# First feed forward: the rows of batches 2 and 3 come back beside the second attention's first groups, in a ring of four buffers

## The chip, the cores and the metric

One core of a Trainium2 chip runs the whole program. The metric is the device time of one execution in microseconds (us), here the median of the runs. Engines: TensorE (PE, matrix products), VectorE (DVE), ScalarE (ACT), GpSimd (POOL) and SyncE (SP, which issues DMAs). Each works through its own queue in order, and semaphores tie the queues together. SBUF is the memory that the engines work in, PSUM (eight banks) receives what TensorE makes.

## What is computed

Four layers on x of shape (4 batches, 1024 rows, 128), each with a layer norm ahead and a residual:

```
x = x + attention_a(layernorm(x))      # 8 heads of 128, relative positions
x = x + feed_forward(layernorm(x))     # 8 experts, top 2
x = x + attention_b(layernorm(x))      # 16 query heads of 8, one key/value head, causal
x = x + feed_forward(layernorm(x))     # the same weights

def feed_forward(x):                   # per row
    scores = softmax(x @ Wg.T);  top 2 of 8, shares renormalised to p1, p2
    for the two experts e:
        a, b = split(x @ W1[e].T + b1[e]);  g = a * sigmoid(b)       # 256 wide
        out += p_e * (g @ Wo.T + bo)
```

## The kernel before

The 4096 rows are 32 tiles of 128 rows (n = 0 to 31), eight to a batch. Three plans, lists of units, give the order: `plan_a` (first attention, with the routing of the first feed forward), `plan_f(0, opening)` followed by the order of the second attention from `plan_b`, and `plan_f(1, [])`. Every engine walks the same list and does its own part of each unit, so the order of the list is the order of each engine's queue.

**The feed forward** sorts rows by expert. `m_disp` scatters normalised rows to DRAM (`xsd`) by an indirect DMA of POOL. `m_load` and `m_turn` bring sorted tiles back and turn them, `m_mm` multiplies a pair of tiles with the expert's weights (TensorE), takes the gate (tanh on ScalarE, m_sig; VectorE, m_gg), and `m_store` writes the pair to DRAM (`gsd`, SP's queue). There are three parts: batches 0 and 1 (20 pairs), batch 2 (12) and batch 3 (12), 44 pairs in all. Then the rows come back, for each tile n:
- `m_gath`: POOL issues two indirect DMAs (one for each of the two experts) into a buffer of a ring. The first gather of a part waits until the part's last four pairs are stored. The ring has `NP` = 7 buffers, and it is the memory of `P`, the attention's probabilities (line 570 on: `self.gb = self.P...`).
- `m_sum`: ScalarE scales the first half (m_acc, line 1215), VectorE adds the second (line 1593). It waits for the gather.
- `m_fin`: TensorE turns m_acc (2 transposes, line 914), ScalarE copies (m_th, 1223), VectorE takes the rest (m_tl, 1598).
- `m_proj`: TensorE multiplies with Wo (6 matmuls, lines 927 to 929), VectorE adds to x (line 1604).

In `plan_f` a set `back(n)` = m_sum n, m_fin n-1, m_proj n-2 follows a pair from pair 24 on, one set for 1.1 pairs. That is sets 0 to 17 by the last pair; the rest stands in a list that `spread` mixes with the opening of the second attention, and the last unit of it is `("b_zero", 1)`, POOL's memset of the key buffer K1. K1 and Q1 lie on the memory of the first feed forward's own buffers (gg, sig, acc, th, tl, xn), so they can be written only when it is through.

**The second attention** has 16 groups (4 batches x 4 groups of 4 heads). The opening makes inputs and keys of batch 0 (`b_in`, `b_keys`), values (`b_vals`), the row maxima of group 0 (`b_max`, 48 of them: TensorE line 1088, VectorE lines 1800 and 1804), and the shift of the queries by them (`b_shift`, `b_shift2`). Group n then has scores (`b_s`, TensorE line 1109), exponentials (ScalarE, 1354), masks (POOL, 760), products with the values (`b_pv`, 1127), and `b_norm`; beside it run the maxima of group n+1 and the inputs of group n+2. `in_order` makes the order: each line of units has due times in groups; of the units that are next in their lines it takes the one with the least idle time by its model of engines, latencies and banks, plus `SLACK` (4000 ns) for each group that it is due later than the earliest. Maxima use banks 0 to 2, scores 3 to 5, products 6, and everything else bank 7.

The second attention's first exponential waits for the last m_sum, since the ring of gathers lies in P:

```
elif nst == 1:
    e.wait_ge(S["b_wlo"], 1)
    e.wait_ge(S["m_sum"], NT)
e.activation(self.P[:, pt, off:512], ps[:, bank, off:512], ACT.Exp).then_inc(S["b_exp"], 1)
```

Of the kernel before, what the change touches and what calls it, by code (L numbers as in the profile page):

```python
# [26 lines left out]
NP = 7  # L27
LATENCY = {"PE": 200, "ACT": 120, "DVE": 150, "POOL": 120, "DMA": 0}
SLACK = 4000.0
NEG = -1e30  # L30
# [146 lines left out]
def plan_f(f, more):  # L177
# [56 lines left out]
def plan_b():  # L234
# [55 lines left out]
    line("scores", tail, 16, 16)  # L290
    rows = disp(1, 0) + disp(1, 1)
# [8 lines left out]
def in_order(lines, due):  # L300
# [5 lines left out]
    def steps(u):  # L306
# [67 lines left out]
        if kind == "m_bias":  # L374
            return [("DVE", 2300, [], [])]
        return [("DVE", 1200, [], [])]
# [14 lines left out]
    def allowed(u):  # L391
# [8 lines left out]
        if kind == "b_in" and u[2] == 4:  # L400
            return ("xb_bias", u[1]) in done
        if kind == "ln_stats":
            return ("b_out2", u[2], 1) in done if u[1] == 3 else True
# [38 lines left out]
class Program:  # L442
# [27 lines left out]
    def memory(self):  # L470
# [93 lines left out]
        self.gb = self.P[:, :, :].rearrange("p s (k n) -> p s k n", k=2)  # L564
        for f in range(2):
            with ExitStack() as c:
# [6 lines left out]
                self.xn8.append(buf("xn", [128, 8, 128]))  # L573
            self.K.append(sb(f"K{1 - f}", [128, 4, L], F32R))
# [208 lines left out]
    def gpsimd_routed(self, e, u):  # L783
# [19 lines left out]
        elif u[0] == "m_gath":  # L803
# [6 lines left out]
            if i == 0:  # L810
                e.wait_ge(S["b_wlo"], 1)
            if i >= NP:
                e.wait_ge(S["m_sum"], i - NP + 1)
            for k in range(2):
                e.indirect_dma_start(self.gb[:, i % NP, k, :], None, self.gsd[part],
                                     bass.IndirectOffsetOnAxis(self.slot[:, k, n:n + 1], 0)).then_inc(self.d_gath[i % NP], 16)
# [351 lines left out]
    def scalar_side(self, e, u):  # L1168
# [40 lines left out]
        elif u[0] == "m_sum":  # L1209
            _, f, n = u  # L1210
            i = NT * f + n
            e.wait_ge(self.d_gath[i % NP], 32 * (i // NP + 1))
# [726 lines left out]
```

## Time and profile before

| what | us |
|---|---|
| median of 3 runs | 2677.29 (2676.71 to 2681.56) |
| profiled execution | 2673.23 |
| its span in the trace | 2671.5 |
| PE busy | 2431.9 (91%) |
| DVE busy | 1891.9 (71%) |
| ACT busy | 1547.2 (58%) |
| POOL busy | 438.9 (16%) |

Stages on the trace's clock: first attention to 1571, first feed forward to 1722, opening of the second attention to 1788, its groups to about 2490, second feed forward to the end.

How to read the rows: "1750.38 0.48 DVE L1593" is a start, a duration, an engine and a line of the kernel. A bracket at the end gives the idle time before it and what ended it. PE is TensorE's matmuls, PEld its weight loads. Matmul records overlap (each is longer than the distance to the next), so a busy PE is not a full one, and the cost of an instruction in a full queue is the distance to the next start. A releaser "remote" is one that the profile can't name. PEclk is the granted clock of TensorE as a share of full speed.

### The profile page before, as it was taken

The numbers are of one execution on the slowest core, as the hardware profiler recorded it, in microseconds if no ns is written. First come the engines' busy times: TensorE is split into PE (matmuls) and PEld (weight loads), VectorE is DVE, ScalarE is ACT, GpSimd is POOL, SyncE is SP. The second block draws the span as 40 slices with busy tenths as digits, with TensorE's granted clock in tenths as the row PEclk, the third lists the DMA queues.
The fourth block names the chain that finished last, engine by engine and source line by source line (L and its number), as shares of the span: only waits on it lengthen the run. The fifth ranks groups of instructions, "written<-read, shape, count | busy, mean of one in ns | idle before, by whom it ended". The sixth has DMA issues, their size and how long they took to land.

```text
span 2671.5 us, 40400 instructions
## 1 busy us (share of the span) xinstructions
PE 2431.9 (91%) x13240; PEld 1878.4 (70%) x13240; DVE 1891.9 (71%) x4726; ACT 1547.2 (58%) x3107; POOL 438.9 (16%) x825
## 2 busy tenths in 40 slices
PE   4999898999999999999999977789999989988776
PEld 3788787788888888888888855665555545544655
DVE  4677776777877778777777754588887877873544
ACT  3566565666766656666566633537766656555333
POOL 0000011000000012000020005422222223423154
PEclk9999999999999999999999987879999989999786
DMA  4666578666666667666577625400000000000363
GB/s 139 238 227 226 185 252 289 212 205 224 230 223 231 206 216 242 213 230 220 200 240 244 225 84 176 147 20 1 1 1 1 1 9 10 24 5 13 110 191 117
DMA packets 171554, 402.51 MB, mean 151 GB/s; under 512 B 28226, under 2 KB 85186, under 8 KB 171010
## 3 DMA queue, kind: packets, MB, share of 16 engines
q1 hardware_dynamic: 154578, 360.38, 40.1%
q0 software_dynamic: 12208, 35.62, 4.3%
q10 hardware_dynamic: 4560, 3.93, 0.5%
q8 instruction: 108, 1.77, 0.3%
q14 instruction: 100, 0.82, 0.1%
HBM read 208.88 MB, written 193.66 MB: 151 GB/s over the span
## 4 chain that ended last, share of the span: by engine, by line
PE 74%; DVE 11%; ACT 5%; issue 4%; another core or an unknown queue 2%; DMA 2%; POOL 1%; SPq 0%; DVEq 0%; ACTq 0%; POOLq 0%
PE ps L1015 7%; PE ps L432 7%; PE ps L434 7%; PE ps L433 7%; PE ps L1088 5%; PE ps L1127 5%; PE ps L990 5%; PE ps L989 5%; PE ps L1109 4%; PE ps L1028 4%; PE ps L1030 4%; PE ps L1029 4%; DVE ps L1800 2%; DVE r_mx L1804 1%
## 5 line engine op out<-in xcount | busy, mean ns | idle before, releaser
L1305 ACT ACTIVATE a_Ph<-ps 128x512 fp32r<-128x512 f32 x512 | 304.9, 596 | 443.0 <-PE ps L1015 440.4
L1354 ACT ACTIVATE r_P<-ps 128x512 f32<-128x512 f32 (+3 forms) x768 | 329.5, 492 | 194.2 <-PE ps L1109 183.0
L1702 DVE CUSTOM_DVE_ANT_0 a_sp<-ps,a_sp 128x1024 f32<-128x1024 f32 x256 | 313.0, 1223 | 144.6 <-PE ps L434 123.6
L1708 DVE TENSOR_TENSOR a_Pl<-ps,a_Ph 128x512 fp32r<-128x512 f32 x512 | 348.8, 682 | 9.8 <-ACT a_Ph L1305 9.8
L989 PE MATMUL ps<-a_fa,a_ua 128*128 128x384 f32 (+2 forms) x960 | 328.0, 354 | 20.5 <-ACT a_rt L1290 18.4
L1298 ACT ACTIVATE a_sp<-a_sp,a_nm 128x1024 f32<-128x1024 f32 x256 | 295.0, 1152 | 50.2 <-DVE a_nm L1702 49.4
L1015 PE MATMUL ps<-ident,a_sp 128*128 128x128 f32 x2048 | 308.9, 274 | 0.0
L1015 PEld LDWEIGHTS ps<-ident,a_sp 128*128 128x128 f32 x2048 | 257.6, 141 | 71.2 <-issue 1.4
L1088 PE MATMUL ps<-r_K,r_Q 128*128 128x512 f32 (+3 forms) x768 | 280.0, 406 | 28.3 <-DVE r_mx L1800 14.3
L990 PE MATMUL ps<-a_fb,a_ub 86*128 86x384 f32 (+2 forms) x960 | 290.7, 318 | 0.0
L1800 DVE CUSTOM_DVE_ANT_0 ps<-ps,r_maskq 128x256 f32<-128x256 f32 (+3 forms) x512 | 244.3, 504 | 38.8 <-PE ps L1088 36.5
L1290 ACT ACTIVATE a_rt<-ps 128x384 f32<-128x384 f32 x512 | 251.1, 490 | 23.3 <-DMA scr<-a_rt 12.7
L1109 PE MATMUL ps<-r_Q,r_K 128*128 128x512 f32 (+3 forms) x768 | 251.5, 383 | 8.7 <-ACT r_P L1354 6.5
L1088 PEld LDWEIGHTS ps<-r_K,r_Q 128*128 128x128 f32 x768 | 145.3, 198 | 145.0 <-DVE r_mx L1800 73.8
L801 POOL DMA_INDIRECT xsd<-m_xd,m_slot x96 | 93.7, 976 | 900.8 <-issue 507.1
L1028 PE MATMUL ps<-a_Ph,a_nath 128*128 128x512 f32 x512 | 215.7, 421 | 27.1 <-DVE a_Pl L1708 26.9
L760 POOL TENSOR_SCALAR_AFFINE_SELECT r_P<-r_P 128x128 f32<-128x128 f32 x512 | 152.5, 309 | 420.4 <-ACT r_P L1354 412.4
L432 PE MATMUL ps<-p_xh,a_gah 128*128 128x512 f32 x512 | 208.3, 407 | 2.5 <-DVE a_ub L1676 1.6
L434 PE MATMUL ps<-p_xh,a_gal 128*128 128x512 f32 x512 | 206.2, 403 | 0.0
L433 PE MATMUL ps<-p_xl,a_gah 128*128 128x512 f32 x512 | 205.5, 401 | 0.0
L989 PEld LDWEIGHTS ps<-a_fa,a_ua 128*128 128x128 f32 x960 | 184.8, 193 | 29.1 <-ACT a_rt L1290 22.4
L1030 PE MATMUL ps<-a_Ph,a_natl 128*128 128x512 f32 x512 | 203.6, 398 | 0.0
(248 smaller groups left out, 4872.9 us busy)
## 6 DMA issues: line engine op xcount, KB each, us to landing
scr<-a_rt SPq DMA_DIRECT2D x256, 576.0 KB
a_sp<-scr SPq DMA_DIRECT2D x256, 512.0 KB, 4.6
gsd<-m_gg SPq DMA_DIRECT2D x82, 256.0 KB
a_share<-rdr SPq DMA_DIRECT2D x64, 256.0 KB, 4.7
a_wc<-wsp SPq DMA_DIRECT2D x24, 512.0 KB, 5.5
m_sx<-xsd SPq DMA_DIRECT2D x38, 256.0 KB
wsp<-a_wc SPq DMA_DIRECT2D x8, 512.0 KB, 5.6
xsd<-in_q POOLq DMA_DIRECT2D x2, 1472.0 KB, 18.5
```

What stands on the lines that cost most here:

```text
L432: e.matmul(out, lh, rh, start=True, stop=False)
L433: e.matmul(out, lh, rl, start=False, stop=False)
L434: return e.matmul(out, ll, rh, start=False, stop=True)
L989: e.matmul(out, self.ua[:, s, side, qs], self.fa[:, base + a:base + z], start=True, stop=False)
L990: i = e.matmul(out, self.ub[:, s, side, qs], self.fb[:, base + a:base + z], start=False, stop=True)
L1015: i = e.transpose(ps[:, 4 + j % 2, 128 * k:128 * k + 128], self.sp[:, (4 * qd + k) % NSP, 128 * j:128 * j + 128], ident[:, :])
L1028: e.matmul(OB, self.nath[:, s, j, :], self.Ph[:, slot, :], start=j == 0, stop=False)
L1088: e.matmul(ps[:, bank, 0:w], self.Q[b % 2][:, g, 128 * I:128 * I + 128], self.K[b % 2][:, q, 512 * part:512 * part + w], start=True, stop= ...
L1109: e.matmul(ps[:, bank, off:512], self.K[b % 2][:, q, 128 * J:128 * J + 128], self.Q[b % 2][:, g, 512 * ch + off:512 * ch + 512], start=Tru ...
L1354: e.activation(self.P[:, pt, off:512], ps[:, bank, off:512], ACT.Exp).then_inc(S["b_exp"], 1)
L1702: e.tensor_tensor_reduce(out=w, in0=ps[:, 2:4, :].rearrange("p a n -> p (a n)"), in1=w, scale=-1.0, scalar=3e38, op0=ALU.add, op1=ALU.min, ...
L1708: e.tensor_tensor(self.Pl[:, n % 2, :], ps[:, 4 + n % 2, :], self.Ph[:, n % 2, :].bitcast(F32), ALU.subtract).then_inc(S["p_lo"], 1)
```

## The change

The gathers of the first feed forward get four buffers of their own (`gb0`, in the memory that K1 and Q1 use later); the second feed forward keeps seven in P. `plan_f(0)` stops at tile 16 (batches 0 and 1). Tiles 16 to 31 come back in a new line "back" of the second attention, due over groups 0 to 2.2, with gathers three tiles ahead and m_fin and m_proj in bank 7; the memset of K1 is its last unit. `in_order` learns costs for these units, and that inputs of batch 1's keys come after the memset. The first exponential no longer waits for m_sum.

```
+NG = (4, 7)
+SPILL = 16
@@ plan_f
+    end = NT if f else SPILL
     for part in range(2):
-        side.setdefault(last[part], []).extend(("m_gath", f, n) for b in PARTS[part] for n in range(8 * b, 8 * b + 8))
+        side.setdefault(last[part], []).extend(("m_gath", f, n) for b in PARTS[part] for n in range(8 * b, 8 * b + 8) if n < end)
     def back(n, fin, proj):
-        return [u for u in (("m_sum", f, n), ("m_fin", f, n - 1, fin), ("m_proj", f, n - 2, proj)) if 0 <= u[2] < NT]
+        return [u for u in (("m_sum", f, n), ("m_fin", f, n - 1, fin), ("m_proj", f, n - 2, proj)) if 0 <= u[2] < end]
-    p += [("m_gath", f, n) for n in range(8 * B - 8, 8 * B)]
-    rest = [u for n in range(nb, NT + 2) for u in back(n, 3 + n % 2, 5)]
+    p += [("m_gath", f, n) for n in range(8 * B - 8, end)]
+    rest = [u for n in range(nb, end + 2) for u in back(n, 3 + n % 2, 5)]
     rest.insert(len(rest) // 2, ("m_bias", f, B - 1))
-    if f == 0:
-        rest.append(("b_zero", 1))
+
+def rows_back(f, lo, ahead):
+    r = [("m_gath", f, n) for n in range(lo, min(lo + ahead, NT))]
+    for n in range(lo, NT + 2):
+        r += [u for u in (("m_sum", f, n), ("m_fin", f, n - 1, 7), ("m_proj", f, n - 2, 7)) if lo <= u[2] < NT]
+        r += [("m_gath", f, n + ahead)] * (n + ahead < NT)
+    return r + [("b_zero", 1)]
@@ plan_b
     line("scores", tail, 16, 16)
+    line("back", rows_back(0, SPILL, 3), 0, 2.2)
@@ in_order: steps
+        if kind == "m_gath":
+            return [("POOL", 2540, [("gb", u[2] % 4)], []), ("DMA", 2600, [], [("got", u[2])])]
+        if kind == "m_sum":
+            return [("ACT", 350, [("got", u[2]), ("acc", u[2] % 2)], [("half", u[2])]),
+                    ("DVE", 400, [("half", u[2])], [("gb", u[2] % 4), ("sum", u[2])])]
+        if kind == "m_fin":
+            return [("PE", 260, [("bank", 7), ("sum", u[2])], [("pe", 0), ("acc", u[2] % 2)]), ("ACT", 320, [("pe", 0)], [("hi", 0)]),
+                    ("DVE", 340, [("hi", 0)], [("bank", 7), ("tl", u[2])])]
+        if kind == "m_proj":
+            return [("PE", 650, [("bank", 7), ("tl", u[2])], [("pe", 0)]), ("DVE", 200, [("pe", 0)], [("bank", 7), ("x", u[2] // 8)])]
+        if kind == "b_zero":
+            return [("POOL", 4000, [], [])]
@@ in_order: allowed
         if kind == "b_in" and u[2] == 4:
-            return ("xb_bias", u[1]) in done
+            return ("xb_bias", u[1]) in done and ("b_zero", 1) in done
@@ gpsimd_routed
-            if i == 0:
-                e.wait_ge(S["b_wlo"], 1)
-            if i >= NP:
-                e.wait_ge(S["m_sum"], i - NP + 1)
+            if n >= NG[f]:
+                e.wait_ge(S["m_sum"], i - NG[f] + 1)
@@ scalar_attention_b
                 elif nst == 1:
                     e.wait_ge(S["b_wlo"], 1)
-                    e.wait_ge(S["m_sum"], NT)
```

The remaining lines of the diff put `self.gb[f][:, n % NG[f], ...]` in the place of `self.gb[:, i % NP, ...]`, count the gathers' semaphores to match, and add two conditions to `allowed` (layer norm of a batch after its rows, `gt_combine` after the memset).

## Rows read from the trace of the kernel before

**Rows 1.** Busy us (and instructions) of each engine by stretch; groups from 1788 on.

```profile
core 0: us, PE busy (x) PEld busy (x) DVE busy (x) ACT busy (x) POOL busy (x), PEclk, DMA share, GB/s
...
1667.00:1722.00 55.00, 45.32 (x238) 36.70 (x238) 34.17 (x96) 26.04 (x58) 28.59 (x30) 0.88 0.54 167
1722.00:1744.00 22.00, 16.22 (x65) 13.74 (x63) 8.32 (x20) 14.36 (x28) 10.06 (x10) 0.56 0.25 73
1744.00:1788.00 44.00, 37.14 (x162) 29.38 (x160) 38.93 (x130) 10.28 (x25) 6.24 (x7) 0.73 0.06 18
1788.00:1827.40 39.40, 37.12 (x219) 21.19 (x218) 34.77 (x118) 26.85 (x59) 13.19 (x36) 0.98 0.00 1
1827.40:1863.00 35.60, 35.27 (x222) 20.58 (x223) 30.47 (x98) 25.24 (x56) 9.38 (x32) 1.00 0.00 1
1863.00:1904.70 41.70, 40.49 (x246) 23.78 (x247) 32.08 (x98) 31.25 (x67) 10.85 (x33) 1.00 0.00 1
1904.70:1939.80 35.10, 34.80 (x215) 19.90 (x216) 28.74 (x93) 24.26 (x55) 9.50 (x32) 1.00 0.01 1
1939.80:1984.50 44.70, 41.91 (x255) 25.01 (x255) 36.97 (x127) 28.93 (x61) 9.84 (x32) 0.96 0.00 1
2260.40:2299.00 38.60, 36.19 (x215) 20.35 (x216) 29.90 (x98) 23.93 (x55) 16.74 (x39) 1.00 0.04 15
```

**Rows 2.** Timeline of VectorE: one m_sum, m_fin, m_proj and the next instruction.

```profile
1687.63 0.48 DVE L1593 SCALAR_TENSOR_TENSOR m_acc<-r_P,m_pw,m_acc 128x256 f32<-128x256 f32 x1
1688.03 0.42 DVE L1598 TENSOR_TENSOR m_tl<-ps,m_th 128x256 fp32r<-128x256 f32 x1
1688.37 0.28 DVE L1604 TENSOR_TENSOR x<-ps,x 128x128 f32<-128x128 f32 x1
1688.56 0.68 DVE L1577 TENSOR_TENSOR m_sxl<-ps,m_sxh 128x512 fp32r<-128x512 f32 x1
```

**Rows 3.** Timelines of ScalarE, then TensorE, in the opening.

```profile
1723.38 0.68 ACT L1327 ACTIVATE r_y<-ps,r_bq 128x512 f32<-128x512 f32 x1
...
1737.46 0.32 PE L432 MATMUL ps<-r_vh,p_xh 128*128 128x8 f32 x1
...
1742.88 1.20 PE L1088 MATMUL ps<-r_K,r_Q 128*128 128x512 f32 x2
...
1788.45 0.31 PE L1109 MATMUL ps<-r_Q,r_K 128*128 128x128 f32 x1
```

**Rows 4.** A wait of 1640:1722, two rows of ScalarE, POOL's DMA queue 1638:1722 (MB).

```profile
ACT m_sig L1208 <- remote: 22.5, 5, 8.1
...
1645.69 0.51 ACT L1215 ACTIVATE m_acc<-r_P,m_pw 128x256 f32<-128x256 f32 x1 [0.65 <-DMA r_P<-gsd,m_slot]
...
1665.86 0.60 ACT L1208 ACTIVATE m_sig<-ps 128x512 f32<-128x512 f32 x1 [8.09 <-remote]
...
q0 software_dynamic: 2246, 6.16, 25.2%
```

**Rows 5.** Timeline of POOL: a gather, the memset of K1, two masks.

```profile
1640.35 1.00 POOL L815 DMA_INDIRECT r_P<-gsd,m_slot  x1 [4.83 <-DMA gsd<-m_gg]
...
1787.48 3.51 POOL L777 MEMSET r_K<- 128x4096 f32 x1 [30.04 <-PE ps L929]
...
1861.39 0.29 POOL L760 TENSOR_SCALAR_AFFINE_SELECT r_P<-r_P 128x128 f32<-128x128 f32 x1 [12.09 <-ACT r_P L1354]
...
1869.80 0.54 POOL L760 TENSOR_SCALAR_AFFINE_SELECT r_P<-r_P 128x128 f32<-128x128 f32 x1 [2.83 <-ACT r_P L1354]
```

**Rows 6.** Timeline of TensorE at full clock: an m_proj, then an m_fin, and what follows.

```profile
1750.91 0.22 PE L927 MATMUL ps<-woh,m_th 128*128 128x128 f32 x1
...
1751.53 0.43 PE L1088 MATMUL ps<-r_K,r_Q 128*128 128x384 f32 x1
...
1752.73 0.38 PE L914 MATMUL ps<-ident,m_acc 128*128 128x128 f32 x2
1752.93 0.44 PE L1088 MATMUL ps<-r_K,r_Q 128*128 128x384 f32 x1
```

More of the change, by code:

```diff
@@ L400, in allowed @@
         if kind == "b_in" and u[2] == 4:
-            return ("xb_bias", u[1]) in done
+            return ("xb_bias", u[1]) in done and ("b_zero", 1) in done
         if kind == "ln_stats":
-            return ("b_out2", u[2], 1) in done if u[1] == 3 else True
+            return ("b_out2", u[2], 1) in done if u[1] == 3 else 8 * u[2] < SPILL or ("m_proj", 0, 8 * u[2] + 7, 7) in done
+        if kind == "gt_combine":
+            return ("b_zero", 1) in done
         if kind == "m_disp":
@@ L563, in memory @@
         self.gg, self.sig, self.acc, self.th, self.tl, self.xn8 = [], [], [], [], [], []
-        self.gb = self.P[:, :, :].rearrange("p s (k n) -> p s k n", k=2)
+        self.gb = []
         for f in range(2):
@@ L573, in memory @@
                 self.xn8.append(buf("xn", [128, 8, 128]))
+                self.gb.append(self.P[:, :, :].rearrange("p s (k n) -> p s k n", k=2) if f else buf("gb", [128, NG[f], 2, FH]))
             self.K.append(sb(f"K{1 - f}", [128, 4, L], F32R))
@@ L809, in gpsimd_routed @@
                     e.wait_ge(self.d_gs[p % 4], 16 * (p // 4 + 1))
-            if i == 0:
-                e.wait_ge(S["b_wlo"], 1)
-            if i >= NP:
-                e.wait_ge(S["m_sum"], i - NP + 1)
+            if n >= NG[f]:
+                e.wait_ge(S["m_sum"], i - NG[f] + 1)
             for k in range(2):
-                e.indirect_dma_start(self.gb[:, i % NP, k, :], None, self.gsd[part],
-                                     bass.IndirectOffsetOnAxis(self.slot[:, k, n:n + 1], 0)).then_inc(self.d_gath[i % NP], 16)
+                e.indirect_dma_start(self.gb[f][:, n % NG[f], k, :], None, self.gsd[part],
+                                     bass.IndirectOffsetOnAxis(self.slot[:, k, n:n + 1], 0)).then_inc(self.d_gath[n % NG[f]], 16)
     def tensor(self, e):
@@ L1211, in scalar_side @@
             i = NT * f + n
-            e.wait_ge(self.d_gath[i % NP], 32 * (i // NP + 1))
+            before = 32 * NT // NG[0] if f and n % NG[1] < NG[0] else 0
+            e.wait_ge(self.d_gath[n % NG[f]], before + 32 * (n // NG[f] + 1))
             if i >= 2:
                 e.wait_ge(S["m_ftr"], i - 1)
-            e.activation(self.acc[f][:, i % 2, :], self.gb[:, i % NP, 0, :], ACT.Copy,
+            e.activation(self.acc[f][:, i % 2, :], self.gb[f][:, n % NG[f], 0, :], ACT.Copy,
                          scale=self.pw[:, n, 0:1]).then_inc(S["m_wsum"], 1)
@@ L1592, in vector_routed @@
             acc = self.acc[f][:, i % 2, :]
-            e.scalar_tensor_tensor(acc, self.gb[:, i % NP, 1, :], self.pw[:, n, 1:2], acc, ALU.mult, ALU.add).then_inc(S["m_sum"], 1)
+            e.scalar_tensor_tensor(acc, self.gb[f][:, n % NG[f], 1, :], self.pw[:, n, 1:2], acc, ALU.mult, ALU.add).then_inc(S["m_sum"], 1)
         elif u[0] == "m_fin":
```

## The prediction, made before the change was run

> **What bounds the kernel now.** I read the busy shares by stretch first [rows 1]. The kernel is four stages on one core: first attention to 1571 us, first feed forward to 1722, second attention, second feed forward. The change touches three stretches. In the late first feed forward (1667 to 1722) TensorE shows 45.3 of 55 us, VectorE 34.2, and the DMA engines a share of 0.54: nothing is full. From 1722 to 1744 nothing is full: it is the latency of the attention's opening (inputs, keys, values). From 1744 to 1788 VectorE is busy 38.9 of 44 us, so it sets the pace with the 48 row maxima of the first group. From 1788 on sixteen head groups follow. The barest one (1904.7 to 1939.8, 35.1 us) has VectorE at 28.7 and TensorE at 34.8; but a busy TensorE here is overlapping records, and its weight loads are busy 19.9 us only. So VectorE and TensorE are both near full and neither alone is.
>
> Next the timelines. Between 1744 and 1788 the rows coming back of the feed forward (m_sum, m_fin, m_proj) stand in VectorE's queue between maxima [rows 2]. The start of the stage is slowed by them too: ScalarE does m_sum between its activations and key copies, and the first maximum is at 1742.88 [rows 3]. The first score of the attention is at 1788.45 [rows 3], just behind the last m_proj. Last, in 1640 to 1722 ScalarE stands still before m_sig for 22.5 us in five spells that the profile ascribes to "remote", the longest of 8.09 us before 1665.86 [rows 4]. Such waits occur only in the two stretches where rows are gathered beside loads and stores.
>
> **Part 1: what leaves the opening (1722 to 1788).** VectorE still has there 14 m_sum, 15 m_fin and 16 m_proj, the last of which are rows 16 to 31. Their price is the distance to the next start, not the duration: 0.40, 0.34 and 0.19 us [rows 2]. From 1743 to the shift it does 10 m_sum, 12 m_fin and 12 m_proj: 10 x 0.40 + 12 x 0.34 + 12 x 0.19 = 10.4 us. In the VectorE-bound part they come off one for one. The last m_proj holds TensorE for six matmuls between the two halves of the shift, 6 x 0.21 = 1.3 us at the low clock. Before 1743: ScalarE's chain is four pairs of activations of about 1.33 us (0.68 at 1723.38 and its copy of 0.63) [rows 3] and eight key copies of 0.64; without m_sum in between and without VectorE waiting for m_acc, two pairs end at 1726.8, four keys at 1729.4, two pairs at 1732.1; the 24 small matmuls of the values take 24 x 0.213 = 5.1 us at the low clock (1737.46 to the first maximum, less one m_fin) [rows 3], from about 1731.5. The first maximum then comes at about 1736.6 and not 1742.9: 6.3 us. Sum of the opening: 10.4 + 1.3 + 6.3 = **18.0 us** gained. Bounds: 13 (half of the latency stays, TensorE's own waits for banks show) to 21 (the idle of VectorE beside the rows, some 3 us, goes as well). The move of the memset of K1 (3.51 us, POOL, 1787.48) [rows 5] out of the start frees the first masks, about 1 us, and costs as much at group 2, where masks queue behind it: nothing.
>
> **Part 2: what arrives in groups 0 to 2.2.** All 16 rows now run there: 16 x (0.40 + 0.34 + 0.19) = 14.9 us of VectorE, and of TensorE 16 x (0.20 for two transposes + 0.62 for six matmuls) = 13.1 us at the full clock [rows 6]; ScalarE gets two activations a row, the longer of 0.51 us [rows 4], so at most 16 us, and has room: 26.9, 25.2 and 31.3 busy in the three groups of 39.4, 35.6 and 41.7 us [rows 1]. These three are VectorE 34.8 + 30.5 + 32.1 = 97.3 busy in 116.7 us, 83.4%. If the planner keeps that share, 14.9 / 0.834 = **17.9 us** are added. Low end: the fuller mix lets it reach the share of group 0, 88.3%: (97.3 + 14.9) / 0.883 = 127.1, or 10.4 us. High end: group 4 against the barest group has 8.2 us more VectorE and takes 9.6 more, 1.17 for one: 17.4 us; and POOL's part from group 11, which has six scattered rows (12 indirect DMAs) and 1.2 us more VectorE and takes 3.5 more [rows 1]: (3.5 - 1.4) / 6 = 0.35 us a row, 16 rows 5.6: together 23. I take 17.9, since the three groups themselves are the nearest rows.
>
> POOL's part: 32 indirect DMAs of 0.95 us with 0.30 between, 2.5 us a row [rows 5], 40 us, beside about 33 us of masks in about 130: it fits, but a mask behind a pair waits up to 2.5 us and the b_pv behind the mask waits on TensorE with all that is queued there. The first three gathers are issued in the opening, where POOL is idle. The added wait (gather n for m_sum n-3, ring of four) comes after it in the order, since gathers are planned three rows ahead; behind it are masks. The DMA engines are idle there (share 0.00) [rows 1].
>
> A mask beside an instruction of VectorE that reads two SBUF tiles takes longer: 0.54 us at 1869.80 while r_yk<-r_yh,r_y runs, against 0.29 [rows 5]. The added m_sum on VectorE reads two SBUF tiles (gb and acc), so up to 16 masks get 0.25 us longer, 4 us of POOL at the very most, mostly hidden. The Trainium skill (SBUF — State Buffer, Who interferes with whom) says the same of VectorE with two SBUF inputs and a GpSimd instruction that reads SBUF: one blocks the other. By that rule as a cost wholly exposed, the gain would be 4 us less; the trace shows the blocking but not that anything waits for it, so the sum leaves it out.
>
> **Part 3: the feed forward, ring of four and not seven.** Before 1722 the kernel summed rows 0 to 17, now 0 to 15: two m_sum and one m_fin leave. Gathers: the software queue moved 6.16 MB by 1722 [rows 4], which is 23.5 rows of 0.262 MB; now 16 rows, 4.19 MB. Less traffic beside loads and stores, and in the burst at 1640 only five rows can be out before m_sum 1, where nine were issued without a pause until 1662.8. The first spells stay (five rows were out then, as they will be); the 8.09 us spell ends when the burst is through, and I let half of it go, 4 us; of the spells after it, 22.5 - 8.1 - 5.1 = 9.3 us at most, 2 us [rows 4]. **6 us** gained, bounds 0 and 14 (8.1 and most of what comes after). Does the ring of four starve the sums? The first gather is issued at 1640.35 [rows 5] and its m_sum starts on ScalarE at 1645.69 [rows 4], 5.3 us later. Rows come at (1722 - 1667) / 16 = 3.4 us each, so four are 13.7 us: cover enough, gone only if a gather takes over 13 us.
>
> The late feed forward has the DMA engines busy at 0.54 while 167 GB/s pass [rows 1]. The Trainium skill (DMA: Bandwidth & Descriptors, Issuing engines are not separate DMA queues) has all DMAs share the same 16 engines whoever issues them, so that 2 MB less would pay in full if these engines were the limit: at that rate 12 us, twice my 6. The share of 0.54 speaks against that as the limit of the whole stretch.
>
> **Sum.** 18.0 + 6 - 17.9 = 6.1 us gained. The profiled execution took 2673.2 us (span 2671.5 and 1.7 around it), 4.1 below the median of the runs, 2677.3. So 2667.1 for a profiled execution, and 2671.2 for the median. A change within 0.2% (5.4 us) can't be told from none.
>
> **Rivals.**
> A, the forecast, 2671: 0.47, of which 0.34 is over 0.2% faster.
> B, paid back in full: the groups take the high price (23 us) and the feed forward gives 2: 18 + 2 - 23 = -3, 2680. For it: the barest group shows no engine with easy room. Against: VectorE-light group 1 took 1.7 us more VectorE for 0.5 us. 0.20.
> C, slower, TensorE stalls on bank 7: in the opening m_fin and m_proj had banks 3, 4 and 5; in the attention both use bank 7, with inputs, shifts and norms. Each m_fin holds it until m_th (0.38) and m_tl (0.42) have run, each m_proj until x is added. TensorE works in order, so a turn that comes too early stops scores and maxima too. Exposed wholly it is 16 x 0.8 = 13 us on top of B's or A's price: 2671 + 13 = 2684. It decides when over half of the turns are exposed, 6.3 us. Against: the order is planned with a model of this bank. 0.14.
> D, the ring of four starves: m_sum waits on ScalarE ahead of the next gate of the feed forward. If each of the last eight rows waits 1 us, and the 6 us are not gained, 2671 + 14 = 2685. It starts where a gather takes over 13 us. 0.07.
> E, more: all of part 3's bound or nearly (14), and the groups fill to 88%: 18 + 14 - 10.4 = 22, 2655. 0.10. The rule of the Trainium skill on shared DMA engines (part 3) points this way.
> F, nothing happens, since the opening waits for something else than rows: the first score at the same time. 0.02.
>
> **How the numbers follow.** Faster by over 0.2%: 0.34 of A and all of E, 0.44. Slower: 0.07 of B, 0.13 of C, 0.05 of D, 0.25. The rest, 0.31. Range: low end 2657 (E but for its best part), high end 2688 (C and D with the 3 us of B); it leaves out about 0.1 on either side. Of the faster cases, A alone spans 2662 to 2677.
>
> **What would show it.** Right: the first maximum about 6 us, the first score about 18 us sooner after the last m_gg; no m_acc in the opening; the time from first score to the end of group 2 up by about 18 us; the later groups unchanged (35.1 us for group 3); the last m_gg of the first feed forward some 6 us earlier. Wrong: groups 0 to 2 up by over 25 us with TensorE waiting for m_tl or x (C) or masks (B); a "remote" or DMA wait before m_acc in the feed forward (D); group 3 longer as well.

## The result and the profile after

The changed kernel takes 2690.34 us (median of 9) against 2677.29 before (median of 9): ratio 1.0042, 95% interval 1.0028 to 1.0056, so 11 us slower by the ratio and 13 by the medians; 2671 was forecast. A "row" is, as in the prediction, one of the 32 tiles of 128 rows. The profiled execution has a span of 2689.4 us (2671.5 before).

Busy time by stretch, as in [rows 1]; the stretches are the late feed forward, the opening to the first maximum and on to the first score, and groups 0, 1, 2, 3:

```profile
core 0: us, PE busy (x) PEld busy (x) DVE busy (x) ACT busy (x) POOL busy (x), PEclk, DMA share, GB/s
1655.00:1709.40 54.40, 46.69 (x244) 38.15 (x244) 35.27 (x98) 26.93 (x60) 20.97 (x22) 0.87 0.51 152
1709.40:1726.00 16.60, 11.08 (x44) 8.80 (x45) 4.00 (x8) 10.43 (x17) 0.00 (x0) 0.74 0.08 25
1726.00:1757.20 31.20, 27.01 (x62) 15.47 (x62) 26.67 (x88) 2.64 (x4) 0.00 (x0) 0.61 0.00 1
1757.60:1820.80 63.20, 51.13 (x259) 31.75 (x258) 45.31 (x146) 32.72 (x74) 31.54 (x56) 0.78 0.15 42
1820.80:1866.70 45.90, 43.66 (x286) 27.49 (x286) 36.90 (x120) 30.41 (x71) 20.16 (x43) 1.00 0.12 36
1866.70:1917.20 50.50, 45.14 (x265) 27.13 (x266) 34.43 (x103) 32.12 (x70) 13.96 (x33) 0.97 0.00 1
1917.20:1952.30 35.10, 34.79 (x215) 19.88 (x216) 28.74 (x93) 24.26 (x55) 9.53 (x32) 1.00 0.01 1
```

Milestones of several kernels are used from here on; each is a start or an end in ScalarE's timeline. "Feed forward" is first to last m_sig, "opening" last m_sig to the first exp, "groups" from the first exp to the output copy that closes group 2.

| profile | feed forward | opening | groups 0, 1, 2 | sum | rest of attention |
|---|---|---|---|---|---|
| before | 142.3 | 67.1 | 38.6 35.6 41.6 | 115.9 | 565.5 |
| before, again (e15) | 119.2 | 69.3 | 39.8 35.6 44.6 | 120.1 | 571.5 |
| after | 130.1 | 48.2 | 63.3 45.9 50.5 | 159.6 | 571.4 |

Three readings. The opening gave what was expected (18.9 us here, 18.0 forecast). Groups 0 to 2 took 43.7 us more, where 17.9 stood in the sum: this is the miss. And the last column shows that the 6 us which the later groups seem to lose are a difference between executions: the kernel before, profiled again, has the same 571 us. The same holds for some 4 us of groups 0 to 2 (115.9 and 120.1 for one and the same kernel; the granted clock of group 2 was 1.00 and 0.92). Below, a difference of under 4 us in that sum is called unclear. Each kernel has one profile, so the ratios of the medians are set beside the profiles where they bear on a reading.

GpSimd at the start of group 0 (timeline; the brackets hold the wait before the instruction):

```profile
1757.94 0.29 POOL L786 TENSOR_SCALAR_AFFINE_SELECT r_P<-r_P 128x128 f32<-128x128 f32 x1 [62.27 <-ACT r_P L1379]
1758.75 0.97 POOL L839 DMA_INDIRECT m_gb<-gsd,m_slot  x1 [0.52 <-issue]
1760.03 1.88 POOL L839 DMA_INDIRECT m_gb<-gsd,m_slot  x1 [0.30 <-issue]
1761.92 0.54 POOL L786 TENSOR_SCALAR_AFFINE_SELECT r_P<-r_P 128x128 f32<-128x128 f32 x2
1762.62 0.96 POOL L839 DMA_INDIRECT m_gb<-gsd,m_slot  x1 [0.16 <-issue]
...
1772.94 0.95 POOL L839 DMA_INDIRECT m_gb<-gsd,m_slot  x1 [0.31 <-issue]
1773.90 1.11 POOL L786 TENSOR_SCALAR_AFFINE_SELECT r_P<-r_P 128x128 f32<-128x128 f32 x4
```

The first mask waits 62.3 us for the first exp, and all gathers stand behind it. The prediction let the first three go out in the idle opening. They don't: they are in the attention's order, not in the opening's, and GpSimd works in order. So ten gathers (five rows; the expectations below, written earlier, say twelve) run between the first masks, within 16 us. One of them takes 1.88 us and not 0.95: it starts beside VectorE's addition of a bias to x (1759.87, below), which reads two SBUF tiles.

TensorE in the same stretch (timeline):

```profile
1761.73 0.79 PE L1112 MATMUL ps<-r_K,r_Q 128*128 128x512 f32 x1 [2.69 <-DVE r_mx L1829]
...
1771.19 0.64 PE L1151 MATMUL ps<-r_P,r_V 128*32 128x256 f32 x8 [1.62 <-POOL r_P L786]
```

VectorE there, and in the end of group 1 and the start of group 2 (timeline):

```profile
1757.66 2.28 DVE L1596 SCALAR_TENSOR_TENSOR x<-m_fbo,p_csum,x 128x128 f32<-128x128 f32 x8
1759.87 1.21 DVE L1788 TENSOR_TENSOR x<-x,r_bvo 128x1024 f32<-128x1024 f32 x1
...
1863.99 0.69 DVE L1825 CUSTOM_DVE_ANT_0 ps<-ps,r_maskq 128x512 f32<-128x512 f32 x1
...
1877.82 0.69 DVE L1829 TENSOR_REDUCE r_mx<-ps 128x1 f32<-128x512 f32 x1 [1.35 <-PE ps L1112]
```

The 2.28 us at 1757.66 are the eight instructions of m_bias of batch 3. Before, it stood among the opening's maxima. Since no row is left to be dealt there, the list `rest` holds m_bias alone, and dealing puts it behind the last shift. Behind it and the bias of x stand the maxima for which TensorE waits 2.7 us, and the granted clock is 0.50 in the first 5 us of group 0 and 0.76 in the next. And from 1864.7 to 1877.8 VectorE has no maximum at all. The planner may not place batch 1's key inputs before the last row and the zeroing of K1, and this rule (the gate, below) makes a part of the pause: the longest pause of the maxima in these groups is 13.1 us here, and 5.3 before, 9.6 in e3 (the same order without the rows) and 5.8 in e5 (without the gate).

No single wait explains the loss. In the three windows of groups 0 to 2 above, TensorE is busy 139.9 of 159.6 us; in the same three of [rows 1] it is busy 112.9 of 116.7. So the busy time grew by 27.0 us, of which 13.1 are the rows' matmuls at the prediction's price, and the idle time by 15.9. TensorE's largest waits in groups 0 to 2, with their total, count and longest:

```profile
PE ps L1112 <- DVE r_mx L1829: 3.9, 4, 2.7
PE ps L1112 <- DVE r_mx L1825: 2.2, 3, 1.8
PE ps L1133 <- ACT r_P L1379: 1.8, 1, 1.8
PE ps L938 <- DVE p_xl L1455: 1.7, 2, 1.1
PE ps L1151 <- POOL r_P L786: 1.6, 1, 1.6
...
PE ps L951 <- DVE m_tl L1623: 0.4, 2, 0.3
```

The waits that end when another unit has done with bank 7 (before m_fin, m_proj, the turns of the outputs and the products of the inputs) are many and short: 15 of them, about 6 us together, the longest 1.15. Before, there was one of 0.4 us.

### The profile page after: what moved, and what is told of

Same layout as the page of the kernel before. It is cut to its first block, busy times and chain, and to the rows that moved or that the text cites. A ratio compares the mean times of both kernels' runs of the same rounds, so it can differ in the third digit from the quotient of the medians.

```text
span 2689.4 us, 40400 instructions
## 1 busy us (share of the span) xinstructions
PE 2444.0 (91%) x13240; PEld 1881.4 (70%) x13240; DVE 1893.2 (70%) x4726; ACT 1547.7 (58%) x3107; POOL 441.9 (16%) x825
## 4 chain that ended last, share of the span: by engine, by line
PE 72%; DVE 11%; issue 7%; ACT 5%; POOL 2%; DMA 2%; another core or an unknown queue 1%; SPq 0%; DVEq 0%; ACTq 0%; POOLq 0%
PE ps L1039 7%; PE ps L457 7%; PE ps L459 7%; PE ps L458 7%; PE ps L1151 5%; PE ps L1014 5%; PE ps L1013 5%; PE ps L1112 5%; PE ps L1133 4%; PE ps L1052 4%; PE ps L1054 4%; PE ps L1053 4%; DVE ps L1825 1%; POOL xsd L827 1%
## 5 line engine op out<-in xcount | busy, mean ns | idle before, releaser
L1013 PE MATMUL ps<-a_fa,a_ua 128*128 128x384 f32 (+2 forms) x960 | 327.8, 354 | 21.1 <-ACT a_rt L1316 18.9
L1825 DVE CUSTOM_DVE_ANT_0 ps<-ps,r_maskq 128x256 f32<-128x256 f32 (+3 forms) x512 | 244.2, 503 | 42.4 <-PE ps L1112 38.0
L1133 PE MATMUL ps<-r_Q,r_K 128*128 128x512 f32 (+3 forms) x768 | 257.4, 391 | 10.3 <-ACT r_P L1379 8.1
L1133 PEld LDWEIGHTS ps<-r_Q,r_K 128*128 128x128 f32 x768 | 144.4, 201 | 91.3 <-ACT r_P L1379 62.7
```

The source lines that it names most:

```text
L1013: e.matmul(out, self.ua[:, s, side, qs], self.fa[:, base + a:base + z], start=True, stop=False)
L1133: e.matmul(ps[:, bank, off:512], self.K[b % 2][:, q, 128 * J:128 * J + 128], self.Q[b % 2][:, g, 512 * ch + off:512 * ch + 512], start=Tru ...
```

## The experiments

Five sets, each on one chip, each against the kernel before there (medians 2674.0, 2675.0, 2621.1, 2622.1 and 2623.1 us; sets 1 and 4 ran on the same chip number). The table is the whole of what they measured; "sum" is groups 0 to 2.

| kernel | set | ratio to before, 95% | feed forward | opening | groups 0, 1, 2 | sum |
|---|---|---|---|---|---|---|
| e1_no_gathers | 1 | 1.0016 (0.9994 to 1.0037) | 130.1 | 47.8 | 54.1 45.3 49.1 | 148.5 |
| e2_no_proj | 1 | 0.9989 (0.9969 to 1.0009) | 130.7 | 48.3 | 53.0 41.4 48.0 | 142.4 |
| e3_order_only | 1 | 0.9954 (0.9934 to 0.9975) | 127.1 | 48.2 | 45.6 40.1 49.1 | 134.8 |
| e4_ring_only | 1 | 0.9985 (0.9959 to 1.0010) | 131.4 | 69.3 | 38.7 35.6 41.6 | 115.9 |
| e5_no_gate | 2 | 0.9935 (0.9910 to 0.9960) | 131.7 | 48.2 | 47.2 39.6 43.1 | 129.9 |
| e6_by_hand | 2 | 1.0088 (1.0071 to 1.0104) | 130.8 | 48.2 | 62.2 55.6 46.7 | 164.5 |
| e7_by_hand_early | 2 | 1.0065 (1.0046 to 1.0083) | 130.9 | 48.0 | 61.0 56.0 50.6 | 167.6 |
| e8_ring_in_P | 2 | 0.9977 (0.9964 to 0.9991) | 136.8 | 70.7 | 40.3 35.6 43.1 | 119.0 |
| e9_tensor_only | 3 | 0.9994 (0.9983 to 1.0004) | 116.4 | 48.2 | 48.2 46.7 42.6 | 137.5 |
| e10_vector_only | 3 | 0.9959 (0.9946 to 0.9972) | 116.9 | 48.2 | 45.5 39.3 41.7 | 126.5 |
| e11_gathers_only | 3 | 0.9988 (0.9975 to 1.0002) | 116.7 | 48.2 | 50.5 40.1 46.5 | 137.1 |
| e12_hand_no_gathers | 3 | 1.0084 (1.0058 to 1.0111) | 116.2 | 46.2 | 60.1 54.0 48.5 | 162.6 |
| e13_hand_empty | 4 | 0.9936 (0.9913 to 0.9960) | 116.3 | 45.8 | 43.5 35.6 43.0 | 122.1 |
| e14_empty_bias | 4 | 0.9908 (0.9885 to 0.9932) | 116.7 | 48.2 | 40.9 35.6 43.0 | 119.5 |
| e15_before_again | 4 | 1.0001 (0.9986 to 1.0016) | 119.2 | 69.3 | 39.8 35.6 44.6 | 120.1 |
| e16_ring_bias | 4 | 0.9991 (0.9978 to 1.0004) | 112.7 | 63.5 | 38.2 35.6 43.1 | 116.9 |
| e17_after_mended | 5 | 1.0017 (1.0004 to 1.0030) | 116.0 | 48.2 | 48.8 43.5 48.2 | 140.5 |
| e18_eight_rows | 5 | 1.0003 (0.9990 to 1.0017) | 116.6 | 58.0 | 44.8 41.8 44.0 | 130.7 |

### Set 1: work left out of the changed kernel, order kept

```
 plan_b():   (each leaves its kinds out of the finished order, for rows 16 to 31)
+    left = ("m_gath",)                                # e1
+    left = ("m_fin", "m_proj")                        # e2
+    left = ("m_gath", "m_sum", "m_fin", "m_proj")     # e3
+    order = [u for u in in_order(lines, due) if not (u[0] in left and u[1] == 0 and u[2] >= SPILL)]
-SPILL = 16
+SPILL = NT                                            # e4: no row in the attention
```

> Leaves out the 32 indirect gathers of rows 16 to 31 of the first feed forward (GpSimd and DMA work); their sums read what the ring of four holds, everything else stands in the order of the changed kernel. Groups 0 to 2 took 115.8 us before and 159.7 us after, 44 more. Theory POOL: the gathers (40 us of GpSimd among masks, 12 of them in a burst at 1758 to 1774 and six at 1795 to 1802) make the excess over the 18 us of VectorE work; groups 0 to 2 fall by 20 us or more, to 140 or less, and TensorE's 'issue' waits of 23 us and the two 'remote' waits of 2 us go back to the 6 us and none of before. Rival ORDER/BANK: the written order and bank 7 make it; they fall by less than 8 us, above 151, and the 10 us at 1867 to 1877 without maxima stay.

> Leaves out m_fin and m_proj of rows 16 to 31 of the first feed forward (two transposes and six matmuls, one ScalarE copy, m_tl and the add to x on VectorE, all uses of bank 7 by these rows); gathers and m_sum stay. Theory BANK: each row holds bank 7 twice and TensorE waits in order; groups 0 to 2 fall by their 16 x 0.53 / 0.834 = 10 us of VectorE and 10 us or more besides, from 159.7 to below 140. Theory POOL: only the VectorE price, about 10 us, goes: near 150. Both: the stall at 1867 to 1877 is gone if it was the chain of the last rows, and stays if the order alone makes it.

> Leaves out all of rows 16 to 31 (gathers, m_sum, m_fin, m_proj), and keeps the order of everything else. Theory WORK (POOL and BANK): the order is not the cost; groups 0 to 2 take what they took before, 115.8 us, within 3. Rival ORDER: batch 1's key inputs stand behind the zeroing of its keys, which stands behind the last row, so VectorE has no maxima in the last part of group 1; 125 us or more even without any row. Either way the time is that of the change with rows for nothing: 2677 - 31 (opening and feed forward) = about 2646 for WORK, 2656 or more for ORDER.

> The ring of four buffers of its own, but all 32 rows back where they were before the change, in the feed forward and the attention's opening. The last m_gg came 12.3 us earlier after the change. Theory RING: the ring of four (fewer gathers in a burst at 1640, no 8-us stall of ScalarE) makes this gain: 2677.3 - 12 = 2665, last m_sig near 1709. Rival ROWS: it came from the two sums and seven gathers that left the feed forward: last m_sig within 3 us of 1721.7, 2675 to 2680.

Leaving the gathers out takes 11 us off the sum, leaving the projections out 17; both values lie between the bounds of the two theories, and neither theory of e1 or e2 holds alone. e3 is the surprise: with no row's work at all the changed order still takes 134.8 us. WORK is refuted; ORDER is right. By the medians e3 is only 12 us faster than before (0.9954), and not 31. e4 shows the feed forward apart: the profile has the 11 us, the medians 4 (and their interval reaches past 1).

### Set 2: what of the order costs

```
 e5 as e3 (no row's work), and the gate taken out of rows_back() and allowed():
-    return r + [("b_zero", 1)]
+    return [("b_zero", 1)] + r
-            return ("xb_bias", u[1]) in done and ("b_zero", 1) in done
+            return ("xb_bias", u[1]) in done
 plan_b(), e6 (no line "back" and none of the change's conditions in allowed(); the order of before, and the rows' 64 steps dealt into it):
+    order = in_order(lines, due)
+    back, until = rows_back(0, SPILL, 3), order.index(("b_in", 1, 4, 0))
+    order = spread(order[:until], back[:-1], 8) + back[-1:] + order[until:]
 plan_f(), e7 as e6, and:
+        p += [("m_gath", f, n) for n in range(SPILL, SPILL + 4)]
+        more = more[:k] + [("m_bias", f, B - 1)] + more[k:]     # k: the first key copy
 e8 as e4, and:
-    buf("gb", [128, NG[f], 2, FH])
+    self.P[:, :, :].rearrange("p s (k n) -> p s k n", k=2)      # with before's two waits
```

> As e3_order_only (no row 16 to 31 at all), but the written order no longer holds batch 1's key inputs back until the last row and the zeroing are in it: the zeroing stands first in its line. e3 took 134.8 us for groups 0 to 2 against 115.8 before. Theory GATE: groups 1 and 2 (4.5 and 7.5 us longer) are the maxima held behind that rule; they fall to within 3 us of before (35.6 and 41.6), group 0 stays at 45, the sum is 122 to 126. Rival DISPLACED: the planner, which thinks of 15 us of row work on VectorE, 13 on TensorE and 40 on GpSimd, puts scores and maxima in a worse order everywhere; the sum stays above 131.

> All work done. The attention's order is that of the kernel before, and the 64 steps of rows 16 to 31 are dealt evenly between its steps, up to the key inputs of batch 1, behind the zeroing. The changed kernel took 159.7 us for groups 0 to 2, of which 19 came with the order and 25 with the work. Theory ORDER: those 19 us can be had back but for the 2.3 us of m_bias; 159.7 - 17 = 143, and 2690 - 17 = 2673 in all. Rival WORK: wherever the rows stand, TensorE waits in order for bank 7 and masks behind gathers; above 155, 2686 or more.

> As e6_by_hand, and the gathers of rows 16 to 19 are issued at the end of the feed forward, where GpSimd and the queue are idle (as the prediction took it), and m_bias of batch 3 stands in front of the first keys, where VectorE is idle. Theory START: eight of the 32 gathers leave the masks (8 x 1.26 = 10 us of GpSimd, of which the 11 us that e1 showed for all gathers give some 3), and m_bias 2.3: groups 0 to 2 at 138, the time 5 us below e6. Rival: GpSimd catches up anyway within group 0; as e6 but for m_bias, 2 us.

> As e4_ring_only, but the ring of four lies in the first buffers of P, as the ring of seven did before, with the two waits that go with that. e4 took 131.4 us from the first to the last m_sig of the first feed forward, before 142.4. Theory DEPTH: four instead of seven buffers make all of the 11 us (fewer gathers out in the burst); 131 to 133 here too. Rival PLACE: the buffers of its own make it (another part of SBUF, no wait for the weights' split); near 142.

e5's 129.9 us lie between the bounds of its two theories. The gate makes 4.9 of the 19 us that e3 has over before, all of it in group 2 (49.1 to 43.1); the rest stays, as DISPLACED has it, but which unit stands wrongly was not tried. But putting the rows evenly into the order of before is no way out: e6 takes 164.5 us and is the slowest of all by its median, so ORDER falls. e7 differs from it by nothing that can be read. In e6 TensorE waits in order for bank 7, for longer than in the changed kernel (total, count, longest):

```profile
PE ps L953 <- DVE m_tl L1625: 4.8, 6, 1.5
...
PE ps L1123 <- DVE m_tl L1625: 1.7, 1, 1.7
PE ps L867 <- DVE m_tl L1625: 1.5, 1, 1.5
```

Only the first of these stands before an m_proj. The others are a shift and a turn of the layer norm that stood behind an m_fin and had to wait for its VectorE step: that is rival C of the prediction, fully, in an order without a planner that knows the bank. e8, the ring of four in the old place, is 0.23% faster than before; its feed forward (136.8 us) lies between that of before and e4, so the two expectations can't be told apart by one profile.

### Sets 3 and 4: each engine's part alone

```
 as e6, and of rows 16 to 31 only:
+    back = [u for u in back if u[0] in ("m_fin", "m_proj") + ("b_zero",)]   # e9, TensorE's part alone
+    back = [u for u in back if u[0] in ("m_sum",) + ("b_zero",)]            # e10, twice m_sum's VectorE step
+    back = [u for u in back if u[0] in ("m_gath",) + ("b_zero",)]           # e11
+    back = [u for u in back if u[0] in ("m_sum", "m_fin", "m_proj") + ("b_zero",)]   # e12
+    back = [u for u in back if u[0] in ("b_zero",)]                         # e13, e14
+        more = more[:k] + [("m_bias", f, B - 1)] + more[k:]                 # e14, e16
 e15: before.   e16: e4 and the line above.
```

> Order of the attention as before, as in e6_by_hand, and of rows 16 to 31 only TensorE's part: two transposes and six matmuls a row into bank 7, on old data, with nobody reading them; no gathers, sums, copies or adds. e6 took 164.5 us for groups 0 to 2, 49 more than before's 115.9. TensorE's price by the prediction's rows is 16 x 0.82 = 13.1 us, and the prediction let it lie beside VectorE's. Theory TENSOR: TensorE, shown busy 113 of 116 us, is full in these groups, and this part costs its whole length: 115.9 + 2.3 (m_bias, now behind the first score) + 13 = 131 or more. Rival BESIDE: it fits into waits for VectorE; below 123.

> Order as e6_by_hand, and of rows 16 to 31 only VectorE's part as two multiply-adds a row on old data (0.40 us each by their distance, 12.8 us in all, for 14.9 of the real row), waited for by nobody. By the prediction's rule (the share of 83.4% is kept) it costs 12.8 / 0.834 = 15: 115.9 + 2.3 + 15 = 133. Theory VECTOR: so, or one for one, 131. Rival SLACK: VectorE's idle 19 us in these groups take it: below 123.

> Order as e6_by_hand, and of rows 16 to 31 only the 32 gathers, each pair waiting for the landing of the pair four rows ahead. In the written order of the changed kernel leaving them out gave 11 us (e1). Theory POOL: a mask behind a pair waits 2.5 us and b_pv behind it; 8 us or more, above 126. Rival HIDDEN: with idle time on the other engines they cost the high bound of the prediction at most, 5.6 us: 118 to 124.

> Order as e6_by_hand, with everything of rows 16 to 31 but the gathers (sums of what the ring holds). Theory CHAIN: sum, transposes, copy, m_tl, matmuls and add follow each other in engines that work in order, and this costs more than TensorE's and VectorE's parts by themselves: e12 less 118 is more than the sum of what e9 and e10 cost, near 155. Rival SUM: it costs what e9 and e10 cost together, or the larger of the two, and the rest of e6's 49 us is the gathers'.

> Order as e6_by_hand, and nothing of rows 16 to 31 (no gather, sum, transpose, matmul, add). It is the base of e6 and of e9 to e12. Theory BASE: only the 2.3 us of m_bias behind the first score come on top of before's 115.9 us for groups 0 to 2: 118 to 119. Rival CLOCK: since TensorE and VectorE have less to do in the opening, and m_bias and the bias of x hold the first maxima, group 0 starts at half clock, and 122 or more.

> As e13_hand_empty, and m_bias of batch 3 stands in front of the first keys, where VectorE waits 3 us for its inputs. Theory BASE: 2.3 us less than e13, 116 for groups 0 to 2, and the opening no longer. Rival CLOCK: more than 3 us less, since TensorE then has no pause of 2.95 us behind the first scores and comes to the full clock earlier.

> The kernel before, unchanged, for a second profile of it beside the ring kernels on this chip. It took 142.3 us from the first to the last m_sig of the first feed forward. If the ring of four is worth 11 us, it is about 11 longer here than e16_ring_bias; if the difference was one of runs and chips, under 5.

> As e4_ring_only (ring of four buffers of its own, all rows back in the feed forward and the opening), and m_bias of batch 3 in front of the first keys and not among the maxima. A version meant to beat both kernels. e4 was 4 us faster than before by the medians; m_bias comes off the VectorE-bound part one for one, 2.3 us: 6.5 us faster, ratio 0.9976. Rival: ScalarE and the rows set the pace there, and m_bias only moves: 4 us, as e4.

The base (e13) is 122.1 us, where BASE said 118 to 119 and CLOCK 122 or more; its group 0 has a granted clock of 0.88 (0.98 and 0.93 in the two profiles of before), so CLOCK is the nearer. It is 2.0 above the second profile of before, which is unclear. From it the parts cost:

| part alone | length | over e13, profile | over e13, ratios of medians x 2622 |
|---|---|---|---|
| VectorE's steps (e10) | 12.8 | **4.4** | 6 |
| TensorE's (e9) | 13.1 | **15.4** | 15 |
| the gathers (e11) | 40 on GpSimd | **15.0** | 14 |
| all but the gathers (e12) | | 40.5 | 39 |
| everything (e6) | | 42.4 | 40 |

The two columns come from different executions and agree within 3 us, though each interval of a ratio is some 3 to 7 us wide on either side. So VectorE's part costs a third to a half of its length (126.5 us is above SLACK's bound of 123 and below VECTOR's 131; the rule of the kept share said 15), and TensorE's costs its whole length and a little more (TENSOR), of which 10.5 us are busy time and 4.9 idle, in part before bank 7. The gathers bear out POOL. Groups 0, 1 and 2 of the base e13 (the columns are those of the windows above):

```profile
1741.10:1784.60 43.50, 39.05 (x215) 22.72 (x215) 37.16 (x126) 27.08 (x60) 10.51 (x35) 0.88 0.00 1
1784.60:1820.20 35.60, 35.27 (x222) 20.58 (x223) 30.35 (x98) 25.23 (x56) 9.46 (x32) 1.00 0.00 1
1820.20:1863.20 43.00, 41.78 (x246) 24.45 (x246) 32.20 (x98) 31.45 (x66) 14.05 (x34) 0.96 0.00 1
```

of e9:

```profile
1746.00:1794.20 48.20, 42.76 (x267) 27.33 (x268) 37.88 (x126) 27.69 (x60) 10.70 (x35) 0.92 0.01 1
1794.20:1840.90 46.70, 42.31 (x286) 27.43 (x287) 31.28 (x98) 25.66 (x56) 9.20 (x32) 1.00 0.00 1
1840.90:1883.50 42.60, 41.55 (x258) 25.06 (x259) 32.06 (x98) 31.36 (x67) 14.34 (x34) 1.00 0.00 1
```

and of e10:

```profile
1743.80:1789.30 45.50, 38.75 (x215) 21.33 (x214) 41.37 (x138) 27.40 (x59) 10.96 (x35) 0.92 0.00 1
1789.30:1828.60 39.30, 37.34 (x222) 20.73 (x223) 36.54 (x116) 25.37 (x57) 10.44 (x31) 1.00 0.00 1
1828.60:1870.30 41.70, 40.49 (x246) 23.66 (x247) 33.28 (x100) 31.21 (x67) 14.53 (x35) 1.00 0.00 1
```

In the base TensorE is busy 116.1 of 122.1 us, and e9 shows that there is next to no room beside it. VectorE has 22 us of room, and e10's share rises from 99.7 of 122.1 (82%) to 111.2 of 126.5 (88%), so the share isn't kept, it rises. e11 has the stall that the prediction had named, since nothing else hides it (wait of TensorE's b_pv for a mask: total, count, longest):

```profile
PE ps L1163 <- POOL r_P L794: 12.0, 7, 3.5
```

Everything but the gathers (e12) costs 40.5 us, twice what its two parts cost alone (19.8): CHAIN. ScalarE's part was not tried alone, so the other 20.7 us belong to the steps following each other through three engines and ScalarE's two activations together. On top of that the gathers cost 1.9 (e6 less e12), nothing that can be read, where alone they cost 15: they don't add to the chain's waits.

e14 gives 2.6 us in the groups for m_bias, about its own length, as BASE has it, and the clock of group 0 rises from 0.88 to 0.90 only. But its opening is 2.4 us longer than e13's (48.2 and 45.8), with the same 107 matmuls at a mean granted clock of 0.62 against 0.74, so the profiles show no gain over the two stretches together. That isn't m_bias: e9 to e11, with m_bias where e13 has it, have 48.2 too. By the medians e14 is 6 to 7 us faster than e13, in intervals that overlap. So what m_bias gives is not settled. e15 and e16 are told apart by 6.5 us in the feed forward, between the two expectations; by the medians e16 is 0.09% faster than before, an interval that takes in 1. Both expectations (6.5 and 4 us) were higher than the 2.4 us that this ratio gives, and it is no gain over e4 (0.9985).

### Set 5: the changed kernel with a mended start

```
 e17: after, planner as it is, and
+        p += [("m_gath", f, n) for n in range(SPILL, SPILL + 4)]        # end of plan_f(0)
+        more = more[:k] + [("m_bias", f, B - 1)] + more[k:]
-    line("back", rows_back(0, SPILL, 3), 0, 2.2)
+    line("back", rows_back(0, SPILL, 4)[4:], 0, 2.2)
 e18: e17 and
-SPILL = 16
+SPILL = 24
```

> The changed kernel with its planner, all work done; the gathers of rows 16 to 19 are issued at the end of the feed forward, as the prediction took it, and m_bias of batch 3 stands in front of the first keys. The changed kernel took 63.3 + 45.9 + 50.5 = 159.7 us for groups 0 to 2. Theory START: the burst of twelve gathers among the first masks and the 2.3 us are gone, groups 0 to 2 fall by 8 us or more, below 152, and the kernel comes within 0.1% of before or under it. Rival TENSOR AND CHAIN: the 16 rows cost what they cost in TensorE's queue; e13 and e14 gave 2.6 us for m_bias, and the gathers only change who waits; 155 or more, ratio 1.002 to 1.004.

> As e17, but only rows 24 to 31 come back beside the attention, over the same stretch (groups 0 to 2.2); rows 16 to 23 stay in the opening. Theory LINEAR: the rows cost what they cost one by one: (159.7 - 122.1) / 2 = 19 us above the base of e13 less m_bias, 119.5 + 19 = 138; the opening gains half, 10 us; ratio 0.9985 + (18 - 10) / 2677 = 1.0015. Rival DENSITY: the waits come from rows that stand close, half as many cost a quarter; 129 or less, ratio below 0.999.

Groups 0, 1 and 2 of e17:

```profile
1743.50:1792.40 48.90, 44.76 (x266) 27.48 (x266) 41.35 (x139) 32.69 (x76) 25.91 (x51) 0.92 0.14 39
1792.40:1835.80 43.40, 42.32 (x278) 26.87 (x278) 37.43 (x119) 30.26 (x70) 18.37 (x41) 1.00 0.11 32
1835.80:1884.10 48.30, 44.23 (x268) 26.89 (x269) 33.79 (x103) 31.70 (x69) 14.35 (x34) 1.00 0.00 1
```

All 16 rows are in these groups of e17, and they take 140.5 us: 19 less than in the changed kernel, 14.5 of it in group 0, whose granted clock goes from 0.78 to 0.92. In its groups START is right (below 152), in its time not: it said within 0.1% of before, and the ratio is 1.0017. Groups 1 and 2 hardly gain (2.4 and 2.3 us); a pause of the maxima of 11.1 us at the start of group 2 is still there. In the first 16.5 us of the group six gathers run, not ten. (In e7 the same start gave nothing: there the rows' chain holds TensorE up wherever they start.) The 16 rows now cost 140.5 - 119.5 = 21.0 us above the empty base e14 in the profiles; by the medians (1.0017 and 0.9908, two sets) 29, and 21 above e13. By the medians the mend is worth less: 1.0017 after 1.0042, 0.25% or 6.7 us, and not 19, with intervals that just touch. Part of the difference lies in the profiled executions: e17's took 2624.96 us, 3.2 under its median, and that of the changed kernel 0.9 over its own. The rest isn't settled; the two were run in different sets. The kernel is still no faster than before.

e18: 130.7 - 119.5 = 11.2 us for eight rows, 1.4 a row, where e17 has 1.3. Neither bound of the expectation was met (138 and 129); both came from the unmended kernel's 38 us for 16 rows. Against e17's 21 a quarter would be 5 us and a half 10.5, so the price is linear, with e17's unit, and DENSITY falls. Opening and groups together take 188.7 us in e17 and in e18, and 183.0 and 189.4 in the two profiles of before: the rows cost no less in the groups than they did in the opening. Time: no difference to before. No version with all work done that was run here beats the ring alone (e8 0.9977, e4 0.9985).

## Why the prediction was wrong

**Opening: right.** 18.0 forecast; 18.9 in the profiles shown, 21.1 against the second profile of before. VectorE's first maximum came 16.7 us after the last m_gg's tanh and not 22.4 (5.6 sooner, 6.3 forecast). But 2.2 of the 18.9 us were m_bias, which had only moved. Its step "the bias of the last batch stays where it is" was never written down; it was taken for granted, and the diff alone (`rest.insert(len(rest) // 2, ...)` with a shorter `rest`) would have shown it.

**Feed forward, 6 us: the size about right, the reason open.** The profiles showed 12.3, the medians of the ring alone 4 and 5 (e4, e8; only e8's interval leaves out 1). The argument hung on ScalarE's "remote" spells [rows 4] as work of the gather burst. In the sets that have them, the length of the feed forward goes with them: before 22.5 us of spells in 142.3, e8 16.0 in 136.8, e4 7.6 in 131.4, the changed kernel 7.5 in 130.1. Less the spells these are 119.8, 120.8, 123.8 and 122.6. But e8 has the same depth of ring as e4 and twice its spells, and in sets 3 to 5 they are gone from the unchanged kernel too (below). So the fewer spells account for the 12 us of the profiles, and that the ring is why they are fewer isn't shown. Without them the ring alone gives 6.5 us (e16, 112.7 for 119.2), and the kernels of sets 3 to 5 with rows moved give 2 to 3, against one profile of before.

The Trainium skill (DMA: Bandwidth & Descriptors, Issuing engines are not separate DMA queues) says that all DMAs share the same 16 engines, and the prediction worked out 12 us from it for 2 MB less traffic, if these engines were the limit. The runs show no such price: the software queue moves 6.06 MB in e17's feed forward and 5.25 in e13's, and they take 116.0 and 116.3 us.

**Groups 0 to 2, 17.9 us: wrong, 43.7 in the profile.** Three steps failed.

First, "the first three gathers are issued in the opening, where POOL is idle". They wait behind the first mask, 62.3 us. With this come the burst of ten among the first masks and a group at 0.78 of the clock. Mended together with m_bias, 19 us of the 43.7 go by the profiles and 7 by the medians; the two mends weren't tried apart in this order.

Second, the price went by VectorE's share, and TensorE's 13.1 us were laid beside it, because "a busy TensorE here is overlapping records". The runs turn this round: VectorE's part is 4.4 us, TensorE's 15.4, and the mended kernel pays 21.0 in all. The forecast of 17.9 was near that by luck, from the wrong engine. That 4.4 and 15.4 add up to nearly 21.0 proves nothing either: in the order by hand, where they were measured, the whole costs 42.4. With 21 in the place of 17.9 the sum reads 18 + 6 - 21 = 3 us gained, which can't be told from none, even with a good start.

Third, "if the planner keeps that share" took the order of everything else as given. The changed order costs by itself, with no row's work in it, 12.7 us over the base e13 (e3; 5 by the medians), 10.6 of them in groups 1 and 2. The gate is 4.9 of it (e5). The prediction had no term for this.

**Rivals.** B had the high price of the groups at 23: the mended kernel pays that, the changed one nearly twice. C (bank 7) is in the changed kernel in part: 0.4 us before m_proj for m_tl, but about 6 us over all 15 waits for the bank, just under the 6.3 at which it was to decide. It is real in e6. D didn't happen: no m_sum waits for a gather in the feed forward longer than before. E and F are out. "Groups up by over 25 us with TensorE waiting for m_tl or masks" was half right as a sign: they were up, but TensorE's waits are spread over more than six reasons and grew by 15.9 us in all. The busy time grew by 27.0, of which 13.1 are new work. The other 13.9 are its old work taking longer or overlapping less. Of the 27.0, 14.0 stand in group 0, where the granted clock is 0.78 against 0.98.

**Open:** why the mend shows 19 us in the profile and 7 in the medians, and how it divides between the early gathers and m_bias; how much of e3's 12.7 us is each of the planner's displacements; what of e12's excess is ScalarE's; whether the ring shortens the spells.

## What to carry to other kernels

Before costing moved work, find its first instruction in the queue of the engine that issues it: a DMA written behind a waiting instruction starts when that one does, however idle the engine is. Price moved work by the engine with the least idle time where it lands, a TensorE that is shown busy included, and try each engine's part alone: here TensorE, whose busy time (116 of 122 us) was taken for mere overlap, charged the whole length, and VectorE at 82% a third to a half. Try the new order with the moved work left out, too: here it cost by itself. Moving work out of a stretch where it costs one for one gains nothing if it lands where it costs the same; and when the lists it was dealt among become empty, look for what else was dealt with them.

## What the runs showed of the hardware

The same kernel, before, took 2677 us in the first measurement, 2674 in set 1 and 2622 in set 4. Its two feed forwards make the difference: in the profiles of the first measurement and of set 4 they take 142.3 and 119.2 us from first to last m_sig in the first, and 153.7 and 126.9 from the end of the attention to the last m_sig in the second. The slower profile has the waits of ScalarE that are ascribed to "remote", 22.5 us before m_sig in the first feed forward alone [rows 4]. The faster one has no row of this kind. All profiles of sets 1 and 2 have such waits, and none of sets 3 to 5 has one in either feed forward, with rings of seven and of four alike. What they are the profile doesn't say; they don't come from this kernel's gathers alone, which were there in both. Sets 1 and 4 ran on the same chip number, 52 us apart by the median of before, so it isn't a property of the chip alone. A feed forward should be compared within one set of runs, with the kernel before profiled in it.
